# Attention stage of a two-layer graph network: accumulator additions one turn later, accumulator numbers read for eight turns at a time

## What is computed

```python
logit = leaky_relu(es[src] + ed[dst], 0.2)          # per edge and head
mx    = segment_max(logit, dst)                     # of the same relation
p     = exp(logit - mx[dst]) * mask
den   = segment_sum(p, dst)
out   = segment_sum(p / den[dst] * x[src], dst)     # per relation
```

## Times and profile before

| | |
|---|---|
| median of 3 runs | 5940.41 us (5938.87, 5940.41, 5980.63) |
| the profiled execution | 5968.85 us, of which its span (first to last instruction) is 5967.0 us |
| attention phase in it | 1828 to 2686 us of the span |
| additions in it | 1028, first 1842.3, last 2684.9 us |
| busy in that phase (858 us) | PE 626, PEld 557, DVE 591, ACT 455, POOL 612 us |
[...]
| DMA in that phase | 0.52 of the 16 DMA engines' time, 128 GB/s |

### The profile page before, as it was taken

The page is one execution under the profiler, slowest core; times in us unless marked ns, Lnnn a source line. Parts: engine busy times, 40 slices in busy tenths (PEclk is TensorE's granted clock), DMA queues, the critical chain, the costliest instruction groups (busy, mean ns, idle before and its releaser), DMA issues. The chain is left out here.

```text
span 5967.0 us, 110677 instructions
## 1 busy us (share of the span) xinstructions
PE 3616.4 (61%) x18587; PEld 2574.6 (43%) x18588; DVE 3898.3 (65%) x11908; ACT 1442.3 (24%) x3070; POOL 3782.6 (63%) x3803
## 2 busy tenths in 40 slices
PE   0153333333314777771558788788778787888877
PEld 0122222222214666661425555555555455555546
DVE  4644444444427666668947777777777777777774
ACT  0120000000004555553332222222222222222222
POOL 3136655565555777765217788888887788878770
PEclk9875565555555555555679999998999999899899
DMA  2254444444423555543157788888887888888874
GB/s 54 62 159 116 111 113 109 114 116 114 108 66 98 130 129 130 130 119 110 47 161 172 173 178 183 178 182 175 180 178 174 179 180 179 179 178 179 178 153 136
DMA packets 895552, 836.72 MB, mean 140 GB/s; under 512 B 228060, under 2 KB 752636, under 8 KB 895257
## 3 DMA queue, kind: packets, MB, share of 16 engines
q0 software_dynamic: 217200, 396.10, 32.2%
q1 hardware_dynamic: 641257, 406.10, 25.1%
q10 hardware_dynamic: 37008, 33.70, 2.4%
HBM read 597.83 MB, written 237.64 MB: 140 GB/s over the span
## 5 line engine op out<-in xcount | busy, mean ns | idle before, releaser
L1543 POOL DMA_INDIRECT sums<-msg_bsum,k_sidx x831 | 1323.3, 1592 | 303.3 <-issue 261.4
L725 POOL DMA_INDIRECT max_xe<-rows,max_idx x832 | 786.1, 945 | 710.9 <-ACT max_idx L797 401.8
L1678 PEld LDWEIGHTS msg_both_ps<-msg_onehot,msg_hid 128*128 128x128 f32 x3712 | 562.4, 208 | 1222.4 <-issue 832.0
L1557 POOL DMA_INDIRECT msg_ga<-ab,k_bsrc x832 | 826.0, 993 | 369.9 <-issue 200.6
L1691 PE MATMUL msg_pre_ps<-msg_rw,msg_lt 128*128 128x512 f32 x1856 | 1047.7, 648 | 8.8 <-DMA msg_rw<-ab 8.8
L1643 ACT ACTIVATE msg_low_ps<-msg_xs 128x512 f32<-128x512 f32 x928 | 558.1, 601 | 2012.7 <-DVE msg_xs L1612 1033.3
L1678 PE MATMUL msg_both_ps<-msg_onehot,msg_hid 128*128 128x64 f32 x3712 | 616.0, 292 | 520.4 <-DVE msg_bsum L1587 338.8
L956 POOL TENSOR_SCALAR att_keyhot<-k_ramp,att_keys 128x128 f32<-128x128 f32 x1028 | 611.6, 611 | 276.2 <-ACT att_keys L1028 276.2
L1611 DVE TENSOR_TENSOR msg_xs<-msg_pre_ps,msg_ga 128x256 f32<-128x256 f32 x928 | 390.8, 421 | 532.1 <-PE msg_pre_ps L1691 219.5
L1622 DVE TENSOR_TENSOR msg_hid<-msg_xs,msg_low_ps 128x512 f32<-128x512 f32 x928 | 637.0, 686 | 106.4 <-issue 40.2
L1068 PE MATMUL att_sum_ps<-att_px,att_keyhot 128*128 128x136 f32 x2056 | 559.0, 453 | 220.5 <-DVE att_px L990 215.3
(11 more groups left out here) (296 smaller groups left out, 6031.3 us busy)
## 6 DMA issues: line engine op xcount, KB each, us to landing
msg_rw<-ab SPq DMA_DIRECT2D x928, 128.0 KB
l_outside<-xe SPq DMA_DIRECT2D x1028, 72.0 KB, 2.5
xe<-max_xe SPq DMA_DIRECT2D x104, 576.0 KB
att_keyrow<-key ACTq DMA_DIRECT2D x257, 128.0 KB, 3.3
msg_lt<-in_efT SPq DMA_DIRECT2D x928, 32.0 KB
rows<-node_rows SPq DMA_DIRECT2D x50, 288.0 KB, 2.4
max_begin<-begin SPq DMA_DIRECT2D x104, 128.0 KB
max_xe<-rows,max_idx POOLq DMA_INDIRECT x832
```

What stands on the lines that cost most here:

```text
L725: pool.indirect_dma_start(xe[:, b, u, :], None, T.rows, bass.IndirectOffsetOnAxis(ap=idx[:, b, u:u + 1], axis=0)).then_inc(s_xe[b], 16)
L1543: pool.indirect_dma_start(T.sums[k % 2], bass.IndirectOffsetOnAxis(ap=K.sidx[:, k:k + 1], axis=0), bsum[:, (k + 1) % SB, :], None, compute ...
L1557: pool.indirect_dma_start(ga[:, (k + 1) % RB, :], None, T.ab, bass.IndirectOffsetOnAxis(ap=K.bsrc[:, k:k + 1], axis=0)).then_inc(s_ga[k % ...
L1678: pe.matmul(fwd_ps[u % 2][:, q * WIN:(q + 1) * WIN], hid[:, b % 2, u, HID + q * P:HID + (q + 1) * P], onehot[:, b, u, :], start=True, stop ...
```

## The change

Two edits, both in DVE's list of `relation_attention`. The additions of a turn are those of group t-6 in place of t-5; everything else in the turn stays where it is. And the loop's body holds eight turns in place of four (2 * RG), on DVE alone, so that one read fetches the window numbers of eight turns, 32. The buffers, and the lists of the other four engines, are the same.

```diff
-            windows = Windows(nc, dve, mybir.EngineType.DVE, K.reg_kw, KWINDOWS - 1, U, RG, 5)
+            windows = Windows(nc, dve, mybir.EngineType.DVE, K.reg_kw, KWINDOWS - 1, U, 2 * RG, 6)
...
             def tick(t, h, has):
                 slot = lambda skew: (h - skew) % RG
-                if has(5):
-                    w = windows.of(t - 5, slot(5))
+                if has(6):
+                    w = windows.of(t - 6, (h - 6) % (2 * RG))
                 for u in range(U):
-                    if has(5):
-                        add(t - 5, slot(5), u, w[u])
+                    if has(6):
+                        add(t - 6, slot(6), u, w[u])
                     if has(4) and u == 1:
                         weigh(t - 4, slot(4))
                     if has(3):
                         select(t - 3, slot(3), u - 1)
 
-            ticks(dve, GROUPS, RG, 5, tick)
+            ticks(dve, GROUPS, 2 * RG, 6, tick)
```

## The result

| kernel | median of 9 runs | lowest to highest | profiled run | its span | granted clock, mean |
|---|---|---|---|---|---|
| before | 5945.22 us | 5932.89 to 5980.63 | 5968.85 us | 5967.0 us | 0.758 |
| after | 6004.23 us | 5991.63 to 6018.77 | 6015.15 us | 6013.3 us | 0.782 |

The ratio is 1.0094, with a 95% interval of 1.0079 to 1.0109. The changed kernel is 59 us slower where 123 us less had been forecast: outside the range, and on the other side. The profiled execution of the kernel before lies 24 us above its median, so the spans differ by 46 us only. The attention phase gained somewhat more than was forecast. The time was lost far behind it, in lines that the change does not touch.

The account below looks back on a forecast made before the run. A circle of waits between DVE's additions and PE's sums was taken to hold the attention phase at 3.295 us a turn; 2.77 over 240 turns saves 126, less 3 for the lost turn: median 5817 us, range 5780 to 5885.

Parts of the forecast that it names:

- The circle and its cut: Attention phase: DVE's additions and PE's sums wait for each other; additions of t-6 cut this, 126 us gained in the loop.
- the lost turn: End of the attention phase: the additions end a turn later, 3 us lost.
- the turns written out: Attention turns outside the loop: they read four numbers each and gain next to nothing; the loop was counted as 240 turns.
- DVE's turns: Attention loop on DVE: 2.39 us without a read, 2.20 for reading 32 numbers, 0.40 branch and setup; 2.72 a turn.
- the 0.05 of coupling: Attention loop: 0.05 us a turn added for DVE's own delays and near misses between engines, making 2.77.
- POOL and SP level with DVE: Attention loop: DVE 2.72, POOL 2.71 (0.4 lost to DVE's weighting) and SP 2.67 us a turn, within 2%.
- POOL becomes the bound: Rival in the attention phase: POOL's keyhots hold the turn; 5877 us, chance 0.15.
- loads of xe come late: Rival in the attention phase: SP's loads land late in DVE's bursts, 0.14 us a turn, 33 us; 5850 us, chance 0.08.
- no effect: Rival in the attention phase: PE's second half waits for add 3 and closes a circle again; about 5940 us, chance 0.06.
- The long read: Rival in the attention loop: 32 numbers cost 7.7 to 8.5 us, as message-phase reads do a number; 5980 us, chance 0.03.
- The step that failed: Whole kernel: the attention phase's 123 us come straight off the total, 5846 us profiled and 5817 us median.
- The last sentence of what would show me wrong: Phases behind the attention: a change of more than 20 us in one of them would refute the prediction.

Follow-up runs that it names:

- e1: Kernel before with only the additions moved to group t-6, DVE's loop kept at four turns; 5533.84 us, ratio 0.9783 to the kernel before.
- e9: Additions of t-6, loop of four, window read behind each weighting, plus POOL's fourth keyhot left out (some sums wrong); ratio 0.9753 to before, attention 701.5 us.
- e12: Changed kernel with 64 idle instructions, plus POOL's fourth keyhot left out (sums of every fourth step wrong); ratio 0.9759 to before, attention 701.9 us.
- e15: Changed kernel with 34 idle instructions behind DVE's attention work, message loop at 2142; 5524.76 us, ratio 0.9765 to the kernel before.
- e7: Changed kernel with 24 idle instructions behind DVE's attention work, message loop at 2132; 5775.36 us, one run.
- e8: Kernel before with 165 idle instructions behind DVE's attention work, message loop at 2080; 5767.63 us, one run.

## Why the prediction was wrong

**The circle and its cut: right.** The wait of 236.2 us is 1.6 us, and the phase gains 135.8 less 1, some 135 us, for 126 less 3. The 12 us more have three sources: the lost turn cost 1 us and not 3, the turns came out a little under 2.77, and the turns written out, put at next to nothing, gained as well (842.6 and 706.8 us are 3.29 and 2.76 us for each of all 256 turns between first and last addition, where the sum counted 240). e1 shows the later additions alone to be 123 us of it.

**DVE's turns: right.** Forecast 2.39 for a turn without a read, 2.20 for the read, 2.72 a turn in all; measured 2.37 to 2.48, 2.10, and 22.1 us from one read to the next (2209.7 to 2231.8), 2.76 a turn, for 2.77 with the 0.05 of coupling.

**POOL and SP level with DVE: right, and not the bound.** POOL loses (708 - 610) x 4 = 0.39 us a turn for 0.4 forecast, a close hit for a term that was a choice between 0.04 and 0.61. Leaving out work of it or of SP gains 1.5 to 6 us; the rivals "POOL becomes the bound" (5877), "loads of xe come late" (5850) and "no effect" (5940) are out. In the 5877 stood 0.1 us a turn for short DVE operations that would hold POOL up; no run shows this term, and what the runs show is the 0.39 in all, with a quarter of the keyhots left out worth 3.9 to 5.5 us of the phase (e9, e12).

**The long read: right to reject.** 32 numbers take 2.10 us, 0.066 each. The read of 19 numbers in the message phase stays at 4.5 us, in the changed kernel too; the price taken from the rows of the same table was the good one.

**The step that failed** is the last one of the sum, which takes the 123 us of the attention phase straight off the whole kernel (5846 for the profiled execution, 5817 for the median). It took a microsecond out of the attention phase as a microsecond out of the kernel, and what the edit does to the instruction list behind that phase was put at nothing, without a reason. What came in its place was a stall at each of the 55 branches of the message loop, 195 us in all. The prediction did not look at the length of the list: 193 instructions more in front of a loop of 315 that branches back 55 times. At hand were the position of the loop in both compiled programs, and the branch's records, which put the first instruction 0.3 us behind it. That another position can cost anything, and how much, no row of before shows, since no stall was in that trace: the runs put it at 277 packets and some 4 us a branch, of which 3.6 us a body, 195 us in all, came through in the result. With a price of 3.6 us a body, the forecast 5817 plus 197 would have been 6014, against 6004 measured. With the 1.2 to 1.6 us of the other chips it would have been a gain.

The last sentence of what would show me wrong, "if a phase behind the attention changes by more than 20 us", is what came; it had no chance of its own among the rivals, and it was the slower side that had been left to the long read alone.

## What to carry to other kernels

An edit that changes the length of an early phase's list moves every loop behind it on that engine: compare where each hot loop's first and last instruction stand in the list before and after. In these runs the loop of 315 paid some 4 us a trip when its first instruction stood at 2080, 2108 or 2132, less what DVE would have waited anyway, and nothing when it stood at 1915, 1921, 2075, 2142 or 2172. Which places are dear was found by moving the loop. A longer unroll for a small saving (11.8 us here) is a poor trade for such a loop (some 60 to 195 us); a few idle instructions ahead of it (34 cost 3 us in e15), or keeping the list's length, brings the gain home (0.9765 in e15, 0.9783 in e1). The count of packets in the instruction queue told the stall in every run here, 350 or 351 for 74 to 77; it does not tell how dear it is, for e7, with two stalls a trip, has 351 as well.

## What the runs showed of the hardware

- In the runs with 350 or 351 packets (loop at 2080, 2108 or 2132) the first instruction stands 4.2 to 4.5 us behind DVE's branch in the middle (5.1 in e8), in those with 74 to 77 packets 0.3 us: 3.9 to 4.3 us more (4.8 in e8). With the loop at 2132 DVE stands still twice a trip (e7, 4.2 and 3.1 us).
- DVE's branch itself takes 63 ns in the runs with the stall and 56 ns in those without it, in the middle (COMPARE_BRANCH rows above).
- In the attention phase the granted clock of TensorE rose from 0.50 to a mean of 0.77, as the stages of the kernel after show (columns as in the earlier trace rows), and its matmuls of the sums became shorter (mean 368 ns after, 1870 to 2560 us, 453 before). The additions wait 1.6 us for them in the whole phase, so the turn does not hang on that:

```profile
1828.00:2560.00 732.00, 498.54 (x3066) 432.54 (x3065) 609.80 (x2339) 453.32 (x1025) 714.76 (x1031) 0.77 0.63 159
```

- The same kernel took 5945 us in the result and 5656 to 5661 us on chips 0, 2, 4 and 9, with the attention phase alike to 0.8 us (842.4 to 842.9 with the additions of before, 706.6 to 707.4 with the change).
